# A mixture-of-experts block: the router on four tiles at a time, a stacked-identity matmul that sums its quarters, and the first expert's weights loaded ahead of the row stores

## What is computed

```python
w = weights[conditions]                       # (32, 64, 64)
xf = einsum('bct,bcd->bdt', x, w).reshape(N, 512)      # N = 2048 rows
gate = softmax(einsum('nh,eh->ne', xf, Wr))   # 8 experts
top2_val, top2_idx = top_k(gate, 2)
flat_idx = concatenate([top2_idx[:, 0], top2_idx[:, 1]])
rank = (cumsum(one_hot(flat_idx)) * one_hot).sum(-1)
w_assign = where(rank <= 640, flat_val, 0)
g = silu(xf @ Wg.T); u = xf @ Wu.T            # per expert, width 352
y = einsum('ne,enh->nh', comb, (g * u) @ Wd.T)
out = x + y
```

## Time and profile before

| | us |
|---|---|
| median of 3 runs | 273.12 |
| lowest, highest | 271.77, 273.74 |
| the profiled execution's own time | 272.44 |
| its span | 270.6 |
| PE busy in the span | 257.8 (95%) |
| DVE, ACT, POOL busy | 161.6, 137.7, 173.6 |

### The profile page before, as it was taken

The page is one execution under the profiler, slowest core; times in us unless marked ns, Lnnn a source line. Parts: engine busy times, 40 slices in busy tenths (PEclk is TensorE's granted clock), DMA queues, the critical chain, the costliest instruction groups (busy, mean ns, idle before and its releaser), DMA issues.

```text
span 270.6 us, 4016 instructions
## 1 busy us (share of the span) xinstructions
PE 257.8 (95%) x1368; PEld 200.0 (74%) x1368; DVE 161.6 (60%) x332; ACT 137.7 (51%) x242; POOL 173.6 (64%) x156
## 2 busy tenths in 40 slices
PE   8999698999999999999999999999999999999991
PEld 4663156999987867888878887777787777878980
DVE  2658998444459664876566639674865867343251
ACT  2356843444464656565366644664565559442100
POOL 5792048741158867884887478858887886685742
PEclk9999979999999999999999999999999999999998
DMA  6996888999869998899679867998899699366441
GB/s 201 363 300 241 344 270 272 386 338 330 294 193 209 202 207 256 162 216 277 170 130 250 238 178 111 200 294 251 154 238 329 148 192 225 40 79 81 131 177 46
DMA packets 27099, 59.00 MB, mean 218 GB/s; under 512 B 6198, under 2 KB 6454, under 8 KB 26976
## 3 DMA queue, kind: packets, MB, share of 16 engines
q1 hardware_dynamic: 16416, 37.89, 44.3%
q0 software_dynamic: 10656, 20.75, 37.2%
HBM read 39.56 MB, written 20.25 MB: 221 GB/s over the span
## 4 chain that ended last, share of the span: by engine, by line
PE 52%; DVE 3%; ACT 2%; DMA 2%; issue 2%; POOLq 0%; ACTq 0%; DVEq 0%
PE bank L1342 19%; PE bank L1429 17%; PE bank L1437 9%; PE bank L1316 3%; DMA xg<-xf_dram,src_turn 2%; PE bank L1444 2%; PE bank L1452 2%; DVE w L1005 1%; ACT hhi L696 1%; POOLq L85 0%; DVE squares L1054 0%; PE bank L1303 0%; DVE hlo L1060 0%; DVE h L1120 0%; DVE h_last L1100 0%
## 5 line engine op out<-in xcount | busy, mean ns | idle before, releaser
L1429 PE MATMUL bank<-xhi,w 128*128 128x512 f32 x280 | 71.6, 398 | 0.0
L1342 PE MATMUL bank<-w,hhi 128*128 128x512 f32 (+1 forms) x216 | 67.1, 393 | 1.5 <-ACT y_sb L667 1.0
L554 POOL DMA_INDIRECT out<-y_sb,dst_row x35 | 56.5, 1613 | 13.4 <-issue 13.4
L1429 PEld LDWEIGHTS bank<-xhi,w 128*128 128x128 f32 x280 | 52.3, 188 | 13.2 <-DVE h_last L1100 0.8
L520 POOL DMA_INDIRECT gate_g<-gates_dram,src_row x40 | 46.8, 1170 | 12.1 <-issue 11.5
L1342 PEld LDWEIGHTS bank<-w,hhi 128*128 128x128 f32 x216 | 39.2, 188 | 10.7 <-DVE hlo L1060 1.6
L1005 DVE TENSOR_TENSOR w<-raw,w 128x704 fp32r<-128x704 f32 (+1 forms) x35 | 37.1, 1060 | 14.6 <-ACT w L609 8.2
L508 POOL DMA_INDIRECT xg<-xf_dram,src_turn x24 | 25.6, 1065 | 26.0 <-DVE xlo L990 11.6
L1342 PE MATMUL bank<-w,hlo 128*128 128x512 f32 (+1 forms) x108 | 41.9, 388 | 0.0
L1437 PE MATMUL bank<-xlo,w 128*128 128x512 f32 x140 | 38.4, 396 | 0.0
L609 ACT ACTIVATE w<-raw 128x704 fp32r<-128x704 f32 (+1 forms) x40 | 36.7, 923 | 0.0
(11 more groups left out here) (138 smaller groups left out, 304.8 us busy)
## 6 DMA issues: line engine op xcount, KB each, us to landing
raw<-wgu SPq DMA_DIRECT2D x32, 352.0 KB, 7.8
xg<-squares SPq DMA_DIRECT2D x24, 256.0 KB, 7.5
x_sb<-x SPq DMA_DIRECT2D x8, 512.0 KB, 7.6
raw<-wd SPq DMA_DIRECT2D x8, 512.0 KB
xf_dram<-xf_sb SPq DMA_DIRECT2D x7, 512.0 KB, 3.0
raw<-wd SPq DMA_DIRECT2D x8, 192.0 KB
out<-x SPq DMA_DIRECT2D x1, 1280.0 KB, 18.3
gate_g<-gates_dram,src_row POOLq DMA_INDIRECT x40, 6.5
```

Source lines behind the costliest of these rows:

```text
L554: nc.gpsimd.indirect_dma_start(out=out[:, :], in_=y_sb[:, n % TPE, :], in_offset=None, out_offset=bass.IndirectOffsetOnAxis(ap=dst_row[:, ...
L1342: last = nc.tensor.matmul(ps[:, cols], left(c), w[:, half, part, o:o + width], start=(c == 0 and q == 0), stop=(closes and c == cs[-1] and ...
L1429: last = nc.tensor.matmul(ACC_BANK[what][:, :], columns(what, k, part), xhi4[:, k, :], start=(k == 0 and part == 0), stop=False)
```

## The change

- The router takes four tiles at a time (`router(g)`, four groups), with 512 moving columns. PE turns eight tiles before the first step, then four, then two. Two DVE and ACT copies of 512 columns, one per group, replace the copies of 256 (groups 0 and 1 on DVE, 2 and 3 on ACT).
- Tiles 14 and 15 are no longer turned on the chip: the host passes them transposed (`xt`, 512 KB), loaded in the queue where the last pair of x was. That last pair is still needed for `condition(14)` and is loaded after the placed rows.
- `quarters` is a 128x8 matrix of four stacked identities. `sum_quarters(g)` multiplies each tile's 128 partial products by it (stationary `xrT`, 8 moving columns, fp32), which turns and sums in one matmul; DVE then only copies 32 columns. It replaces `turn` and `xr_sum`.
- Logit groups are of four tiles each; the last two are ranked together.
- No `condition` stands among the router's steps. `condition(0)` and `condition(2)` come after `logits(3)`, the other six after the rank matmuls.
- The exponentials are one instruction after xf copy 13; the gates' sums are ahead of `src_row`, their product after it.
- All five weight units of expert 0 are loaded before the row stores; their high and low parts are made after the last xf copy and after the lists; `src_turn` moves behind the first `x_low`. KEEP_WARM is 25. The first expert waits for two low units, then for four.

```diff
-LG = ((0, 3), (3, 5), (5, 7), (7, NM))
+LG = ((0, 2), (2, 4), (4, 6), (6, NM))
-KEEP_WARM = 18
+KEEP_WARM = 25
@@ sync
-            for m in range(2, NM):
+            for m in range(2, NM - 1):
                 load_x(m)
-            sp.dma_start(xf_dram[N:N + 1, :], x[0:1, :]).then_inc(xf_out, 16)
-            sp.dma_start(gates_dram[N:N + 1, :], x[0:1, 0:E]).then_inc(gates_out, 16)
+            sp.dma_start(turned_x[:, RING:RING + 2, :, :],
+                         xt.rearrange("p (r k c) -> p r k c", r=2, k=KH)).then_inc(xt_in, 16)
...
             for j in range(HALF, TT):
                 place(j)
+            load_x(NM - 1)
+            sp.dma_start(xf_dram[N:N + 1, :], x[0:1, :]).then_inc(xf_out, 16)
+            sp.dma_start(gates_dram[N:N + 1, :], x[0:1, 0:E]).then_inc(gates_out, 16)
...
-            for u in range(KH):
+            for u in range(NU):
                 load_unit(0, u)
...
-            load_unit(0, KH)
@@ tensor
+            def router(g):
+                for j in range(g * XR, min((g + 1) * XR, TURNED)):
                     turned(j)
+                if g == NG - 1:
+                    pe.wait_ge(xt_in, 16)
+                if 1 <= g < NG - 1:
+                    pe.wait_ge(xrT_ok, g)
                 for k in range(KH):
+                    if g < NG - 1:
+                        last = nc.tensor.matmul(ps_xrT[g][k * Q:(k + 1) * Q, :]
+                                                .rearrange("q (j c) -> q j c", j=XR),
+                                                wr_sb[:, k, :],
+                                                turned_x[:, g * XR:(g + 1) * XR, k, :],
+                                                start=True, stop=True)
+                    else:
...
+            def sum_quarters(g):
+                pe.wait_ge(quarters_ok, 1)
+                pe.wait_ge(xrT_ok, g + 1)
+                if 1 <= g < NG - 1:
+                    pe.wait_ge(xr_ok, g)
+                for j in range(XR):
+                    last = nc.tensor.matmul(ps_xr[g][:, j * E:(j + 1) * E],
+                                            xrT[:, g % 2, j * P:(j + 1) * P], quarters[:, :],
+                                            start=True, stop=True)
                 last.then_inc(xr_ps, 1)
...
+            turn_tiles(0, 8)
+            pe.wait_ge(wr_in, 16)
+            router(0)
+            turn_tiles(8, 12)
+            router(1)
+            sum_quarters(0)
+            turn_tiles(12, TURNED)
+            sum_quarters(1)
+            logits(0)
+            router(2)
+            logits(1)
+            router(3)
+            sum_quarters(2)
+            sum_quarters(3)
             logits(2)
             logits(3)
-            after = EARLY_PAIRS * 2 + BEFORE_RANKS
-            for j in range(EARLY_PAIRS * 2, after, 2):
-                condition(j)
+            condition(0)
+            condition(2)
...
-            for j in range(after, TT, 2):
+            for j in range(4, TT, 2):
                 condition(j)
@@ scalar
+            for g in range(XRT_DVE, NG):
+                act.wait_ge(xrT_ps, g + 1)
+                nc.scalar.activation(xrT[:, g % 2, :], ps_xrT[g][:, :],
+                                     ACT.Copy).then_inc(xrT_ok, 1)
...
+            for n in range(TT):
+                xf_copy(n, n % XR)
+                if n == TT - 3:
+                    act.wait_ge(sub_ok, 2)
+                    nc.scalar.activation(ex[:, :, :], lg[:, :, :], ACT.Exp).then_inc(ex_ok, 1)
+            for u in range(KH):
                 w_high(u, 0, 0)
...
+            w_high(KH, 0, 0)
             x_high(0)
-            w_high(KH, 0, 0)
@@ vector
+            nc.vector.reduce_sum(quarters[:, :], ident[:, :].rearrange(
+                "p (k c) -> p c k", k=KH)[:, 0:E, :], AX).then_inc(quarters_ok, 1)
+            for j in TURN_DVE[0:4]:
+                turn_copy(j)
+            xrT_copy(0)
+            for j in TURN_DVE[4:]:
+                turn_copy(j)
+            xrT_copy(1)
+            xr_copy(0)
+            xr_copy(1)
+            top_two(0)
+            top_two(1)
+            xr_copy(2)
...
             one_hot(0)
-            top_two(2)
-            top_two(3)
-            subtract(GATED, LG[3][0] * 2)
+            xr_copy(3)
+            top_two(2, 3)
             subtract(LG[3][0] * 2, TT)
             one_hot(1)
-            gates(1)
+            subtract(0, LG[3][0] * 2)
```

More of the change, by code:

```diff
@@ L967, in _ @@
                                     ALU.add).then_inc(lists_ok, 1)
[L968 removed]
+            gates()
+            for u in range(KH):
                 w0_low(u)
[L971 to L977 removed]
             def x_low(s):
```

189 lines of the change are left out of this document (71 added, 118 removed).

## The result

The changed kernel takes 278.64 us (median of four runs, 275.77 to 279.91) beside 272.50 of the kernel before in the same comparison: ratio 1.0206, 95% interval 1.0107 to 1.0305. That is 6.1 us slower by the medians, where I had forecast 1.6, and outside the range. A later comparison gave 278.93 (277.40 to 280.07) and 1.0192 [1.0133, 1.0251]. In all comparisons here the medians are of all executions, while the ratios leave out the slow ones (most of them over 1.5% above the fastest of the same kernel), so a ratio can be lower than that of the medians.

A forecast was written before the change was run, and what follows sets the result against it. The prediction took the chain last xf copy, last row store, gather, experts as the bound: +2.2 for the copy less 0.45 for the gather gave +1.75, and 274.7 us was forecast, range 272.2 to 276.4.

The forecast's parts named there:

- What bounds the kernel: Chain from last xf copy through last row store and gather to the experts; lists second by 1.06 us.
- The price of the matmul with `quarters`: Router on PE: 1.05 us per group of four tiles, bounds 0.56 and 1.5.
- End of the router: PE's routing order: logits 2 and 3 done at 24.8 us, against 24.90 before.
- The last copy: xf copies on ACT: the last ends at 35.7 us, 2.2 later than 33.46.
- copy + 4.1: Row stores: the last lands 4.1 us after the last xf copy, at 39.8.
- supply and DMA agree: Row stores: 10.3 us of bytes from 27 with about 1 us of gap also end at 39.5.
- Weights ahead of the stores cost nothing: Expert 0's weights on DMA: through by about 26 us, before the first store is ready.
- I had 0.45: First gather, no longer beside the down weights: 0 to 0.9 us shorter, taken as 0.45.
- done at 42.3; the tile arrives at 43.8. Free: 25 KEEP_WARM matmuls ahead of the experts: 5.3 us from about 37, no cost.
- The clock rival: TensorE clock falls in the routing (about 1 us) or under KEEP_WARM (up to 278.4): 276.5 us, chance 0.13.

The follow-up runs named there:

- clock kept: Changed kernel with fill matmuls while PE waits for x and between the last router steps, and 36 KEEP_WARM matmuls: 277.57 us, ratio 1.0114.
- order only: Kernel before with conditions 0 and 2 behind the last logits and the ranks ahead of the third condition pair: 276.29 us against 273.91, ratio 1.0099.
- down back: Changed kernel with x-wait fill matmuls, 30 KEEP_WARM, transposes for `quarters`, conditions 0, 2, 4 earlier, down weights behind row stores: 275.20 us, ratio 1.0057.
- fill: Changed kernel with twelve unread matmuls of 256 columns added between the last router steps: 278.62 us, ratio 1.0207.
- 36 KEEP_WARM: Changed kernel with 36 instead of 25 KEEP_WARM matmuls: 276.26 us, ratio 1.0104.

## Why the prediction was wrong, point by point

- **What bounds the kernel:** right. The gather was released by a row store, ahead of which the lists were ready by 3 us; PE ran through the experts but for the clock.
- **The price of the matmul with `quarters`:** right. 2.02 us for two groups, 1.01 each, where I took 1.05. Against transposes they cost 1.1 us of the routing (clock kept), so they are a loss, not a saving.
- **End of the router:** predicted 24.8, measured 24.35, and 24.95 with the clock kept and twelve fill matmuls. Right.
- **The last copy:** +2.2 predicted, +2.63 with the clock kept. Right in mechanism, 0.4 short: the `quarters` are 1.1 of it (against transposes), and the order alone costs 1.07 (order only). In the changed kernel it is +4.16; the other 1.5 are the clock's, which made the first two condition pairs and the ranks slow: the first copy came 2.11 us after the first condition's load instead of 1.19.
- **Stores ("copy + 4.1", "supply and DMA agree"): this term was too small.** The way from the last copy to the gather took 4.51 and 4.72 us in the two executions of the changed kernel and 5.74 with the clock kept, where I had carried over 4.09. The second ground that I gave does not add up: 27 + 10.3 us of bytes + 1 us of gap is 38.3, not 39.5. What I had not seen is that the landing of the last store varies: 3.2 or 3.3 us in the kernel before, with its down weights first, and in down back, and 3.7 to 5.6 us in all other executions. Late and packed stores are not shown to be the whole reason (clock kept, above). Nor does the time from the first store to the gather decide it: it was 13.6 to 14.8 us in the eight executions with late stores, but 14.3 in the kernel before too.
- **Weights ahead of the stores cost nothing:** right, but only because the copies are late. Putting them back gained nothing in the changed kernel. With early copies they cost 1.94 us at the gather's start and give 1.1 back in the gather. In the change the gather got shorter by 0.32, and by 0.84 with the clock kept; I had 0.45.
- **KEEP_WARM 25 "done at 42.3; the tile arrives at 43.8. Free": wrong, and the step that I should have seen.** A pause of 1.5 us stood in my own forecast. It became 2.15, and the clock fell on the first twelve products: +1.34 us. With eleven more matmuls it did not fall there. I had looked at what happens if the KEEP_WARM matmuls run low and end late, not at what their end leaves open.
- **The clock rival** had a chance of 0.13 and named two places. Its low stretch in the routing came, and cost 1.5 us at the last copy, not about 1; but not behind the longer wait for x, after which the clock stayed up (that wait was 1.25 us, at 10 us). Its other place, KEEP_WARM itself at the low level, was the wrong one: those matmuls ran at the upper level, ended early, and the clock fell behind them. That the time lay nearest to this rival's 276.5 is so partly luck.

What the clock costs in the routing can be read from the last copy. In the executions of the changed order that were low somewhere in the routing it ended at 36.74 to 38.29 (at 36.30 with the conditions put forward); in those that were not, fill and clock kept, at 35.98 and 36.09, although these have 12 and 28 matmuls more.

The sum of the changed kernel's own execution, against the forecast of +1.75: last copy +4.16 (forecast 2.2), way to the gather +0.42 (0), gather -0.32 (-0.45), behind the first tile +0.94 (0), together 5.2 us. So the steps that failed are the clock, put at nothing in the routing and behind KEEP_WARM (about 1.5 and 1.3 us), and with smaller parts the last copy (0.4) and the landing of the stores (0.4). With the clock kept the same sum is 2.63 + 1.65 - 0.84 - 0.34 = 3.1 us. The difference of 2.1 us is 1.53 at the last copy, 0.52 in the gather and 1.28 behind the first tile, less 1.23 on the way to the gather, which took longer with the clock kept. By the ratios the change loses 2.0% (1.0206 and 1.0192) and 1.1% with the clock kept; these intervals overlap.

Still open: what makes the clock fall in the routing. In the changed kernel PE had been busy for 1.00 of 1.00 us just before it fell, in matmuls with few columns; with filling there it did not fall in three executions out of four, but in others without filling it did not either, and the low stretch stood at 11 to 16 us instead. Also open is what sets the landing of the last store, why one gather takes 3.6 us and another 5.2 with an idle DMA, and the time behind the first tile: without a low clock there it was 228.2 to 231.3 us, with one 229.5 to 232.3.

## What to carry to other kernels

When a change moves the transfers of a stage, do not carry over "last producer plus so much" as one number. Split it into the last transfer's issue, its landing and the start of what waits for it, and look how much the landing varies between transfers: here 3.2 to 5.6 us for the last store of 256 KB. Work out the end from all the bytes as well, and write down every term of that sum. When filler work keeps a clock up, ask what comes between its end and the real work, and when in doubt make it a little too long: a gap of 2 us cost 1.3 us here. A surplus costs itself, though: next to nothing in 36 KEEP_WARM, about 0.6 us in down back. An instruction put off to "after the others" on the engine that feeds a slower one (here the conditions that feed the copies and the stores) is paid at the end of that slower chain, even where its own engine gains: 1.07 us at the last copy in order only.

## What I had not expected of the hardware

- PE reads as busy in 6.00 of 6.00 us from 24 to 30 while its granted clock is 0.50. Busy time by itself does not tell that the clock is up.
- The landing of the last store comes well behind the bytes. With the clock kept the DMA share was 0.55 from 38 to 40 and 0.03 from 40 to 42; the store landed at 41.1 and the gather was issued at 41.83. For about two microseconds hardly more than one of the sixteen engines was at work, but for the short store of the gates.
- A gather of one tile landed 3.5 to 4.2 us after its issue with the DMA engines nearly idle, and once 5.1 with nothing beside it; beside the down weights it took 4.0 to 4.7 us. Its first issue on GpSimd took 1.0 to 2.6 us.
- The profile's row can name the wrong releaser: in order only it names `dst_row`, whose count the gather does not wait for.
